# The second attention of a four-stage kernel: projections in halves between the heads, scores two heads at a time, loops written out

## The chip, the cores and the metric
The kernel runs on one core of one Trainium2 chip. The metric is device time in microseconds (us) of one execution. Engines: TensorE (PE), VectorE (DVE), ScalarE (ACT), GpSimd (POOL) and SyncE (SP), each with its own instruction stream; they order each other by semaphores.

## The reference
Two layers on x of 8 x 256 x 256 (batch, token, feature): recurrent scans, attentions and expert networks. The part that the change touches is the attention of the second layer, on the output of an LSTM scan, with 8 heads of 32 query and key features:

```python
xn = (x - mu) * jax.lax.rsqrt(var + LN_EPS) * gamma + beta
q = (xn @ Wq + bq).reshape(B, S, H, dk).transpose(0, 2, 1, 3)
k = (xn @ Wk + bk).reshape(B, S, H, dk).transpose(0, 2, 1, 3)
v = (xn @ Wv + bv).reshape(B, S, H, D).transpose(0, 2, 1, 3)
scores = jnp.einsum('bhsd,bhtd->bhst', q, k) / jnp.sqrt(jnp.asarray(dk, x.dtype))
p = jax.nn.softmax(scores, axis=-1)
att = jnp.einsum('bhst,bhtd->bhsd', p, v)
out = att.reshape(S, B, D, H).sum(axis=-1).reshape(B, S, D)
```

The last line sums eight neighbouring columns of the value product, so the kernel sums eight columns of `Wv` beforehand and a head's values have 32 columns.

## The kernel before, in words
`build_kernel` (L2058) runs `pipeline_one` (a scan of the first layer, its attention and experts, and the LSTM of the second layer), `attention_two` (L988), and `pipeline_two` (a gated scan and its experts). Only `attention_two` is touched.

**Precision.** Every float32 operand of a large product is split in two float16 parts, high and low (`_h`, `_l`, `_hi`, `_lo`); a product is three matmuls (high by high, and the two mixed ones). `split_matmul` (L98) issues six for two blocks of 128 contracted features.

**LayerNorm block (L1060 to L1175).** Four pieces of 512 columns: PE forms means and variances with a constant matrix, ACT squares and takes roots, DVE does the rest, POOL adds beta into `hs1`. DVE and ACT also split the projection weights. DVE's memsets stand at its start.

**A block between (L1186).** SP sets the semaphores to a start value for one batch that does not exist; PE writes 12 small matmuls into `pt` and `po`. The loops below begin with heads of that missing batch, so waits need no special case.

**The attention block (L1204 on).** Each engine runs `Fori(0, B)` over 8 batches, with the heads written out inside; waits compare with `at(b, per, k)`, computed in registers.

- PE, per head h: `scores` (L1273), six matmuls of 32 rows and 256 columns into `sc[h % 2]`; `turn` (L1285) of head h-1, four float32 transposes of the probabilities into `pt`; `values` (L1297) of head h-3, twelve matmuls of 32 columns into `po`. At h = 0, scores stand last. At h = 4, `project` (L1249) forms q, k and v of the next batch: 42 matmuls, six of them a bias over 2 rows, in three banks `pq`, `pk`, `pv`.
- ACT: `exps` (L1332), two exponentials with row sums; `high` (L1341), the float16 copy of the turned probabilities, of head h-2; at h = 0 the high parts of q and k, at h = 2 of v.
- DVE: the row maximum (L1412), negated into `nmax`; `low` (L1375), the remainder after `high`, of head h-2; at h = 0 the low parts of q and k and the reciprocals of the sums; at h = 2 `finish` (L1385) of the batch before, the low part of v, and `split_x` (L1369), two instructions that split the next batch's columns of `hs1` into `xn_h`, `xn_l`.
- POOL, beside them: twelve pieces of the next stage's weights, each a DMA, a scaling, a cast and a subtraction (L1214 to L1228).
- SP sends a finished batch to memory (L1243).

q, k, v, their parts and `xn` exist once, so q and k of a batch are read out at its start, after the last scores of the batch before.

## Time and profile before

| | us |
|---|---|
| median of 3 runs | 2952.01 |
| lowest and highest | 2944.11 and 2957.39 |
| the profiled execution | 2941.34 |
| its span, first to last instruction | 2939.5 |
| in the span: `pipeline_one` | 0 to 1417 |
| LayerNorm block and block between | 1417 to 1471.4 |
| attention block | 1471.4 to 1757 |
| `pipeline_two` | from 1761 |

Over the span PE is busy 2524.8 us (86%), DVE 1973.6 (67%), ACT 1149.9 (39%), POOL 430.8 (15%). The page's row of PE's granted clock reads 9 (0.9 or more of full speed) for most slices and falls to 5 and 6 around the second attention. Full speed is 2.4 GHz and 0.50 is 1.2 GHz, the two levels that occur; a figure between is a mean over time. Durations of matmuls overlap: the distance of two starts tells what one costs in a row of them.

### The profile page before, as it was taken

The numbers are of one execution on the slowest core, as the hardware profiler recorded it, in microseconds if no ns is written. First come the engines' busy times: TensorE is split into PE (matmuls) and PEld (weight loads), VectorE is DVE, ScalarE is ACT, GpSimd is POOL, SyncE is SP. The second block draws the span as 40 slices with busy tenths as digits, with TensorE's granted clock in tenths as the row PEclk, the third lists the DMA queues.
The fourth block names the chain that finished last, engine by engine and source line by source line (L and its number), as shares of the span: only waits on it lengthen the run. The fifth ranks groups of instructions, "written<-read, shape, count | busy, mean of one in ns | idle before, by whom it ended". The sixth has DMA issues, their size and how long they took to land. (4 is left out here: it accounts for less than half of the span.)

```text
span 2939.5 us, 119767 instructions
## 1 busy us (share of the span) xinstructions
PE 2524.8 (86%) x50858; PEld 2074.4 (71%) x50858; DVE 1973.6 (67%) x7388; ACT 1149.9 (39%) x3661; POOL 430.8 (15%) x404
## 2 busy tenths in 40 slices
PE   1678999999999999885377874899999999999999
PEld 0455677777777777643144543899999999999998
DVE  4557777777777777875745443667677666776665
ACT  3125555555555555562233432233333333333333
POOL 0000000000000000000189100122222222222222
PEclk9678999999999999997656565899999999999999
DMA  5000000000000000000122003000000000000000
GB/s 159 1 2 2 5 5 5 5 5 5 5 5 5 5 5 5 6 4 3 37 97 86 7 16 112 20 8 8 8 9 8 8 10 8 9 11 8 5 5 6
DMA packets 52730, 53.55 MB, mean 18 GB/s; under 512 B 24679, under 2 KB 46840, under 8 KB 50042
## 3 DMA queue, kind: packets, MB, share of 16 engines
q1 hardware_dynamic: 47284, 27.79, 3.5%
q0 software_dynamic: 2000, 14.68, 1.4%
q8 instruction: 390, 6.39, 0.9%
q10 hardware_dynamic: 2934, 3.69, 0.4%
q14 instruction: 122, 0.99, 0.1%
HBM read 39.59 MB, written 6.55 MB: 16 GB/s over the span
## 5 line engine op out<-in xcount | busy, mean ns | idle before, releaser
L103 PE MATMUL p<-g_hl,m_h 128*128 128x128 f16 x3072 | 529.2, 219 | 0.0
L103 PE MATMUL p<-g_hh,m_l 128*128 128x128 f16 x3072 | 529.1, 219 | 0.0
L103 PE MATMUL p<-g_hh,m_h 128*128 128x128 f16 x3072 | 529.1, 219 | 0.0
L765 DVE STREAM_TRANSPOSE gt<-lg_b 128x512 f32<-128x512 f32 x324 | 230.4, 711 | 217.0 <-PE lg_b L448 203.7
L1910 POOL TENSOR_TENSOR a_l<-a,a_h 128x384 f16<-128x384 f32 x256 | 234.1, 914 | 918.2 <-ACT a_h L1868 918.2
L657 ACT ACTIVATE hm<-xy,b 128x512 f32<-128x512 f32 x512 | 348.0, 680 | 0.1
L642 ACT ACTIVATE gl<-gt 128x128 f32<-128x128 f32 x324 | 100.2, 309 | 629.0 <-DVE gt L765 628.9
L103 PEld LDWEIGHTS p<-g_hh,m_h 128*128 128x128 f16 x3072 | 300.5, 98 | 1.8
L103 PEld LDWEIGHTS p<-g_hh,m_l 128*128 128x128 f16 x3072 | 300.7, 98 | 0.7
L103 PEld LDWEIGHTS p<-g_hl,m_h 128*128 128x128 f16 x3072 | 300.9, 98 | 0.0
L448 PE MATMUL lg_b<-a_wh_hi,lh 128*32 128x256 f16 x4096 | 217.7, 291 | 78.8 <-DVE lh L789 76.7
L448 PE MATMUL lg_b<-e_wh_hi,lh 128*32 128x256 f16 x4096 | 210.5, 283 | 46.3 <-DVE lh L789 45.6
L448 PEld LDWEIGHTS lg_b<-a_wh_hi,lh 128*32 128x32 f16 x4096 | 101.2, 100 | 160.4 <-DVE lh L789 129.3
L1794 PE MATMUL po<-m_h,a_h 128*128 128x256 f16 x768 | 208.4, 271 | 1.9 <-DVE acc L1949 1.9
L1794 PE MATMUL po<-m_h,a_l 128*128 128x256 f16 x768 | 209.0, 272 | 0.0
L1794 PE MATMUL po<-m_l,a_h 128*128 128x256 f16 x768 | 208.8, 272 | 0.0
L1858 ACT ACTIVATE cand<-g_b 128x16 f32<-128x16 f32 x256 | 47.1, 184 | 384.6 <-PE g_b L1758 384.6
L614 PE MATMUL yo<-hm,w2f 128*32 128x256 f32 x2048 | 161.9, 389 | 35.2 <-DVE tmp L815 35.0
L2024 DVE SCALAR_TENSOR_TENSOR zm<-zr,cand 128x16 f32<-128x16 f32 x256 | 44.4, 173 | 206.1 <-ACT cand L1858 205.0
L1868 ACT ACTIVATE a_h<-a 128x384 f16<-128x384 f32 x256 | 133.9, 523 | 105.8 <-DVE a L1933 105.8
L1736 PEld LDWEIGHTS g_b<-g_hh,gu_w 128*128 128x128 f16 x4096 | 136.7, 96 | 51.7 <-DVE g_hh L2029 46.5
L1736 PE MATMUL g_b<-g_hh,gu_w 128*128 128x8 f16 x4096 | 140.5, 166 | 37.1 <-DVE g_hh L2029 35.9
(421 smaller groups left out, 7105.5 us busy)
## 6 DMA issues: line engine op xcount, KB each, us to landing
m_stage<-in_m_w POOLq DMA_DIRECT2D x12, 1024.0 KB, 5.3
hs<-in_m_w SPq DMA_DIRECT2D x16, 384.0 KB, 3.2
xs<-in_x POOLq DMA_DIRECT2D x1, 2048.0 KB, 8.5
x_dram<-x SPq DMA_DIRECT2D x16, 128.0 KB, 2.2
s_v<-in_l_wv SPq DMA_DIRECT2D x1, 2048.0 KB
attention_dram<-att SPq DMA_DIRECT2D x16, 128.0 KB, 2.8
attr<-attention_dram SPq DMA_DIRECT2D x128, 16.0 KB, 1.8
x2r<-x_dram SPq DMA_DIRECT2D x16, 128.0 KB, 2.5
```

The source lines that it names most:

```text
L103: ins = pe.matmul(out, w[wp](k), x[xp](k), start=start, stop=last and k == KT - 1 and xp == 1, skip_group_check=True)
L448: last = pe.matmul(gate_block(ae, j, par), lh[:, part, ae, k, u, :], columns(w[name], k, j), start=False, stop=(part == 1 and k == KT - 1) ...
L614: last = pe.matmul(yo[q * HD:(q + 1) * HD, :, :], w2f[:, n % E1, :], tok[:, :, q, :], start=True, stop=True, skip_group_check=True, tile_p ...
L642: act.activation(gl[:, :].rearrange("p (m b) -> p m b", b=B), gt[:, :].rearrange("p (m n) -> p m n", n=32)[:, :, slot % QS * B:(slot % QS ...
L657: act.activation(hm32[:, n % 2, h * 512:(h + 1) * 512], xy[h][:, :], ACT.Gelu, bias=b1[:, n % E1:n % E1 + 1], scale=1.0 / S).then_inc(g_32, 1)
L765: dve.transpose(gt[:, :], lg_b[slot // QS % 2][:, :, :, :].rearrange("p g a x -> p (g a x)"))\
L1736: pe.matmul(o[:, slot % 8, m, :], w[:, k, m * P:(m + 1) * P], h(g_hh, k), start=False, stop=False, skip_group_check=True)
L1794: last = pe.matmul(po[:, half, :], x[:, n % 2, r], w[:, tl, :], start=(first and x is a_h and w is m3_h), stop=(end and x is a_l), skip_gr ...
L1858: act.activation(cand[:, :], g_b[slot // 8][:, slot % 8, 4:6].rearrange("p m b -> p (m b)"), ACT.Tanh, scale=1.0 / S).then_inc(u_act, 1)
L1868: act.activation(a_h[:, n % 2, :], a32[:, n % 2, :], ACT.Copy).then_inc(a_hi, 1)
L1910: pool.tensor_tensor(a_l[:, n % 2, :], a32[:, n % 2, :], a_h[:, n % 2, :], ALU.subtract).then_inc(a_lo, 1)
L2024: dve.scalar_tensor_tensor(out=zm[:, :], in0=zr[:, 0:16], scalar=1.0, in1=cand[:, :], op0=ALU.add, op1=ALU.mult).then_inc(z_mix, 1)
```

## The change
Loops over batches are written out, and waits compare with constants; the block between, its seeds and its dummy matmuls are gone, as is the projection of a ninth batch. Heads are numbered through, g = 0 to 63, in 32 pairs.

- `scores(p)` treats heads 2p and 2p+1: twelve matmuls, alternating between two row groups (r0 and r0 + 32) and two of four banks `sc`. It is issued in even heads.
- `project(b, j, half)` forms half of q, k or v (7 matmuls). `PROJECT_AT` puts the halves behind heads 0, 1, 3 (two), 5 and 6. All but the first batch use one bank, `pj`; a projection's first half waits for the low part of the one before (`pj_lo`).
- The bias matmuls contract over 128 rows, all but two of them zero.
- `xn`, q, k, v and their parts, and `sums`, are doubled; `split_x` works two batches ahead, high part at h = 4, low part at h = 6.
- ACT puts `high(g-1)` behind `exps(g)`; DVE has `low(g-2)` and the maximum of head g+2, before other work in odd heads and after it in even ones.
- In the LayerNorm block squares go to `prob`, `yy` to `att`, y replaces the root in place, seven memsets go and one of `brow` comes.

```diff
+GH = B * NH
+
+PROJECT_AT = {0: ((0, 0),), 1: ((0, 1),), 3: ((1, 0), (1, 1)), 5: ((2, 0),), 6: ((2, 1),)}
+HIGH_AT = {2: 0, 4: 1, 7: 2}
+PJ_SCALE = (float(DK) ** -0.5 / S, 1.0 / S, 1.0 / S)
...
-        brow = sb("brow2", [2, 3 * D], F16)
-        ones2 = sb("ones2b", [2, BT], F16)
+        brow = sb("brow2", [P, 3 * D], F16)
+        ones2 = sb("ones2b", [P, BT], F16)
...
-        nmax = sb("nmax", [P, 2, TT])
+        nmax = sb("nmax", [P, 4, TT])
         prob = sb("prob", [P, 2, TT, BT])
-        sums, rinv = sb("sums", [P, NH, TT]), sb("rinv", [P, NH, TT])
+        sums, rinv = sb("sums", [P, 2, NH, TT]), sb("rinv", [P, NH, TT])
         pt_h, pt_l = sb("pt_h", [P, 2, TT, BT], F16), sb("pt_l", [P, 2, TT, BT], F16)
...
-        sc = [ctx.enter_context(nc.psum_tensor(f"sc{j}", [P, TT, BT], F32)) for j in range(2)]
+        sc = [ctx.enter_context(nc.psum_tensor(f"sc{j}", [P, TT, BT], F32)) for j in range(4)]
         pt = [ctx.enter_context(nc.psum_tensor(f"pt{j}", [P, TT, BT], F32)) for j in range(2)]
         po = ctx.enter_context(nc.psum_tensor("po", [P, NH, TT, HV], F32))
-        pq, pk, pv = (ctx.enter_context(nc.psum_tensor(n, [P, TT, BT], F32)) for n in ("pq", "pk", "pv"))
+        pj = ctx.enter_context(nc.psum_tensor("pj", [P, TT, BT], F32))
+
+        def pj_bank(b, j):
+
+            return (sc[2], sc[3], pj)[j] if b == 0 else pj
...
+                dve.memset(brow[:, :], 0.0).then_inc(ready, 1)
                 dve.memset(ones2[:, :], 1.0)
-                dve.memset(hs1[:, :, (NI + 1) * CW:(NI + 1) * CW + B], 0.0)
-                dve.memset(sums[:, :, :], 1.0)
-                for tl in (prob, pt_h, pt_l):
-                    dve.memset(tl[:, :, :, :], 0.0)
-                for tl in (v_h, v_l):
-                    dve.memset(tl[:, :, :], 0.0)
...
+                    v, y = va[:, j % 2, :], root[:, j % 2, :]
...
-                        o = bank[:, m, :]
-                        pe.matmul(o, brow[0:2, j * D + m * P:j * D + (m + 1) * P], ones2[0:2, :], start=(m == 0),
-                                  stop=False, skip_group_check=True)
...
+            def project(b, j, half):
+
+                bank = pj_bank(b, j)
+                if half == 0:
+                    pe.wait_ge(xn_split, 2 * (b + 1))
+                    if b > 0:
+                        pe.wait_ge(pj_lo, 3 * b + j)
+                o, xh, xl = bank[:, half, :], xn_h[b % 2], xn_l[b % 2]
+                r = slice(half * P, (half + 1) * P)
+                if j < 2:
+                    n = "qk"[j]
+                    pe.matmul(o, brow[:, j * D + half * P:j * D + (half + 1) * P], ones2[:, :], start=(half == 0),
+                              stop=False, skip_group_check=True)
+                    last = split_matmul(pe, o, (lambda k: w_hi[n][:, k, r], lambda k: w_lo[n][:, k, r]),
+                                        (lambda k: xh[:, k, :], lambda k: xl[:, k, :]), False, last=True)
+                else:
+                    pe.matmul(o, ones2[:, 0:P], brow[:, 2 * D:3 * D], start=(half == 0), stop=False,
                               skip_group_check=True)
-                    w = (lambda k, u=u: xn_h[:, k, u * P:(u + 1) * P], lambda k, u=u: xn_l[:, k, u * P:(u + 1) * P])
-                    last = split_matmul(pe, o, w, (lambda k: w_hi["v"][:, k, :], lambda k: w_lo["v"][:, k, :]), False,
+                    last = split_matmul(pe, o, (lambda k: xh[:, k, r], lambda k: xl[:, k, r]),
+                                        (lambda k: w_hi["v"][:, k, :], lambda k: w_lo["v"][:, k, :]), False,
                                         last=True)
-                last.then_inc(proj_pe, 1)
...
+            def scores(p):
+
+                b, m, r = p // 4, p % 4 // 2, 2 * DK * (p % 2)
+                if p % 4 == 0:
+                    pe.wait_ge(pj_lo, 3 * b + 2)
+                if p >= 2:
+                    pe.wait_ge(exp_done, 2 * (2 * p - 2))
+                elif p == 1:
+                    pe.wait_ge(pj_lo, 3)
+                qh, ql, kh, kl = (v[b % 2] for v in (q_h, q_l, k_h, k_l))
...
+                    for q, k in ((qh, kh), (ql, kh), (qh, kl)):
+                        for e in range(2):
+                            r0 = r + e * DK
+                            last = pe.matmul(sc[2 * (p % 2) + e][:, s_, :], q[r0:r0 + DK, m, s_ * P:(s_ + 1) * P],
+                                             k[r0:r0 + DK, m, :], start=(s_ == 0 and k is kh and q is qh),
+                                             stop=(k is kl), skip_group_check=True, tile_position=(r0, 0))
                 last.then_inc(sc_pe, 1)
 
-            def turn(b, h):
-                pe.wait_ge(exp_done, at(b, 2 * NH, 2 * (h + 1)))
-                pe.wait_ge(pt_lo, at(b, NH, h + 1))
+            def turn(g):
+                pe.wait_ge(exp_done, 2 * (g + 1))
+                if g >= 2:
+                    pe.wait_ge(pt_lo, g - 1)
...
+                pe.wait_ge(pt_lo, g + 1)
                 if h == 0:
-                    pe.wait_ge(v_split, at(b, 1, 1))
-                    pe.wait_ge(att_done, at(b, 1, 1))
-                hd = h % NH
+                    pe.wait_ge(pj_lo, 3 * b + 3)
+                    if b > 0:
+                        pe.wait_ge(att_done, b)
+                vh, vl = v_h[b % 2], v_l[b % 2]
...
-            project(0)
-            with pe.Fori(0, B) as b:
-                for h in range(NH):
-                    if h > 0:
-                        scores(b, h)
-                    turn(b, h - 1)
-                    values(b, h - 3)
-                    if h == 0:
-                        scores(b, h)
-                    if h == 4:
-                        project(b + 1)
-            turn(B, -1)
-            for h in (-3, -2, -1):
-                values(B, h)
+            for j in range(3):
+                for half in range(2):
+                    project(0, j, half)
+            scores(0)
+            for g in range(GH + 2):
+                b, h = g // NH, g % NH
+                if 1 <= g <= GH:
+                    turn(g - 1)
+                if g % 2 == 0 and g // 2 + 1 < GH // 2:
+                    scores(g // 2 + 1)
+                if g >= 2:
+                    values(g - 2)
+                for j, half in PROJECT_AT.get(h, ()):
+                    if b + 1 < B:
+                        project(b + 1, j, half)
...
+            def exps(g):
+                b, h = g // NH, g % NH
+                act.wait_ge(neg_max, g + 1)
+                if g >= 2:
+                    act.wait_ge(t_pe, g - 1)
+                if h == 0 and b >= 2:
+                    act.wait_ge(r_done, b - 1)
...
+            def high(g):
+                act.wait_ge(t_pe, g + 1)
+                if g >= 2:
+                    act.wait_ge(pv_pe, g - 1)
+                act.activation(flat(pt_h[:, g % 2]), flat(pt[g % 2][:, :, :]), ACT.Copy).then_inc(pt_hi, 1)
+
+            def projected(b, j):
+                act.wait_ge(pj_full, 3 * b + j + 1)
+                if b >= 2 and j < 2:
+                    act.wait_ge(sc_pe, 4 * (b - 1))
+                elif b >= 2:
+                    act.wait_ge(pv_pe, NH * (b - 1))
+                act.activation(flat((q_h, k_h, v_h)[j][b % 2][:, :, :]), flat(pj_bank(b, j)[:, :, :]), ACT.Copy,
+                               scale=PJ_SCALE[j]).then_inc(pj_hi, 1)
...
+            for j in range(3):
+                projected(0, j)
+            for g in range(GH + 1):
+                b, h = g // NH, g % NH
+                if g < GH:
+                    exps(g)
+                if g >= 1:
+                    high(g - 1)
+                if h in HIGH_AT and b + 1 < B:
+                    projected(b + 1, HIGH_AT[h])
...
+            def split_x(b, part):
+
+                o = (LAG + 1) * CW
+                row = hs1[:, :, o:o + NCH * CW].rearrange("p k (t b) -> p k t b", b=B)[:, :, :, b]
+                if part == 0:
+                    if b >= 2:
+                        dve.wait_ge(pj_full, 3 * (b - 1))
+                    dve.tensor_scalar(xn_h[b % 2][:, :, :], row, 1.0, None, ALU.mult).then_inc(xn_split, 1)
+                else:
+                    dve.wait_ge(xn_split, 2 * b + 1)
+                    dve.tensor_tensor(xn_l[b % 2][:, :, :], row, xn_h[b % 2][:, :, :],
+                                      ALU.subtract).then_inc(xn_split, 1)
...
+            def projected(b, j):
+                dve.wait_ge(pj_hi, 3 * b + j + 1)
+                hi, lo = ((q_h, q_l), (k_h, k_l), (v_h, v_l))[j]
+                dve.scalar_tensor_tensor(out=lo[b % 2][:, :, :], in0=pj_bank(b, j)[:, :, :], scalar=PJ_SCALE[j],
+                                         in1=hi[b % 2][:, :, :], op0=ALU.mult, op1=ALU.subtract).then_inc(pj_lo, 1)
+
+            def row_max(g):
+                dve.wait_ge(sc_pe, g // 2 + 1)
+                if g >= 4:
+                    dve.wait_ge(exp_done, 2 * (g - 3))
+                dve.tensor_reduce(nmax[:, g % 4, :], sc[g % 4][:, :, :], AX_X, ALU.max,
+                                  negate=True).then_inc(neg_max, 1)
+
+            def low(g):
+                dve.wait_ge(pt_hi, g + 1)
+                dve.tensor_tensor(pt_l[:, g % 2], pt[g % 2][:, :, :], pt_h[:, g % 2], ALU.subtract).then_inc(pt_lo, 1)
...
+            split_x(0, 0)
+            split_x(0, 1)
+            for j in range(2):
+                projected(0, j)
+            row_max(0)
+            row_max(1)
+            projected(0, 2)
+            split_x(1, 0)
+            split_x(1, 1)
+            for g in range(GH + 2):
+                b, h = g // NH, g % NH
+                if 2 <= g:
+                    low(g - 2)
+                if g % 2 == 1 and g + 2 < GH:
+                    row_max(g + 2)
+                if h == 0 and b > 0:
+                    inverse(b - 1)
+                    if b < B:
+                        projected(b, 2)
+                elif h == 1 and b > 0:
+                    finish(b - 1)
+                elif h in (3, 5) and b + 1 < B:
+                    projected(b + 1, h // 2 - 1)
+                elif h in (4, 6) and b + 2 < B:
+                    split_x(b + 2, h // 2 - 2)
+                if g % 2 == 0 and g + 2 < GH:
+                    row_max(g + 2)
```

On PE, before, behind head 4 of a batch (`sc` scores, `pt` the turn, `po` values, `pq` the projection of q):

```order
L1280 MATMUL sc0<-k_h,q_h 128x256
L1280 MATMUL sc0<-k_h,q_l 128x256
L1280 MATMUL sc0<-k_l,q_h 128x256
...
L1291 MATMUL pt1<-ident2,prob 128x128 x4
L1307 MATMUL po<-v_h,pt_h 128x32
L1307 MATMUL po<-v_l,pt_h 128x32
...
L1251 ISA
L1257 MATMUL pq<-ones2b,brow2 128x256
L103 MATMUL pq<-xn_h,q2_hi 128x256
L103 MATMUL pq<-xn_h,q2_lo 128x256
```

and in the changed kernel, heads 4 and 5 of the first batch (`pj` here the first half of v of the second):

```order
L1285 MATMUL pt1<-ident2,prob 128x128 x4
L1273 MATMUL sc2<-k_h0,q_h0 128x256
L1273 MATMUL sc3<-k_h0,q_h0 128x256
L1273 MATMUL sc2<-k_h0,q_l0 128x256
L1273 MATMUL sc3<-k_h0,q_l0 128x256
...
L1303 MATMUL po<-v_h0,pt_h 128x32
...
L1285 MATMUL pt0<-ident2,prob 128x128 x4
...
L1251 MATMUL pj<-brow2,ones2b 128x256
L103 MATMUL pj<-v2_hi,xn_h1 128x256
```

The scores of two heads stand matmul by matmul beside each other and come once in two heads, and the projection is cut in pieces between heads.

On DVE, before, from head 2 to head 3 of a batch (`pt_l` the low part, `nmax` the row maximum):

```order
L1412 TENSOR_REDUCE nmax<-sc0 128x2
L1377 TENSOR_TENSOR pt_l<-pt0,pt_h 128x512
...
L1390 TENSOR_TENSOR att2<-po,rinv 128x512
...
L1418 SCALAR_TENSOR_TENSOR v_l<-pv,v_h 128x512
...
L1371 TENSOR_SCALAR xn_h<-hs1 128x512
L1372 ISA
L1373 TENSOR_TENSOR xn_l<-hs1,xn_h 128x512
...
L1412 TENSOR_REDUCE nmax<-sc1 128x2
```

and in the changed kernel, heads 3 to 6 of the first batch:

```order
L1392 TENSOR_REDUCE nmax<-sc1 128x2
L1385 SCALAR_TENSOR_TENSOR q_l0<-pj,q_h0 128x512
L1397 TENSOR_TENSOR pt_l<-pt0,pt_h 128x512
L1376 TENSOR_SCALAR xn_h1<-hs1 128x512
L1392 TENSOR_REDUCE nmax<-sc2 128x2
L1397 TENSOR_TENSOR pt_l<-pt1,pt_h 128x512
L1392 TENSOR_REDUCE nmax<-sc3 128x2
L1385 SCALAR_TENSOR_TENSOR k_l0<-pj,k_h0 128x512
L1397 TENSOR_TENSOR pt_l<-pt0,pt_h 128x512
L1379 TENSOR_TENSOR xn_l1<-hs1,xn_h1 128x512
```

The two x-split instructions no longer follow each other, and the low parts of q and k stand behind a row maximum.

## Rows read from the trace of the kernel before

**Rows 1.** Stretches, core 0: us, then busy us and instructions by engine, PEclk, DMA

```profile
core 0: us, PE busy (x) PEld busy (x) DVE busy (x) ACT busy (x) POOL busy (x), PEclk, DMA share, GB/s
...
1626.00:1660.00 34.00, 30.79 (x215) 19.80 (x214) 14.22 (x23) 12.11 (x39) 0.07 (x1) 0.50 0.05 8
...
1800.00:2939.50 1139.50, 1091.56 (x22474) 1044.27 (x22474) 774.64 (x3001) 352.79 (x1087) 234.10 (x256) 0.97 0.05 13
```

**Rows 2.** The same view, for projection, heads alone, heads afterwards, the whole stage

```profile
1643.00:1654.00 11.00, 11.00 (x47) 5.57 (x46) 0.52 (x1) 0.00 (x0) 0.00 (x0) 0.50 0.00 0
1699.00:1705.00 6.00, 6.00 (x48) 4.30 (x47) 4.58 (x7) 2.27 (x7) 0.00 (x0) 0.50 0.27 39
...
1746.70:1756.00 9.30, 6.88 (x108) 5.51 (x106) 5.53 (x9) 5.12 (x16) 0.00 (x0) 1.00 0.00 0
...
1471.40:1757.00 285.60, 227.50 (x1826) 151.02 (x1826) 138.15 (x190) 110.99 (x348) 144.97 (x48) 0.62 0.17 51
```

**Rows 3.** Waits from 1493 to 1748: us in total, times, longest

```profile
DVE nmax L1412 <- PE sc L1280: 115.7, 36, 12.1
```

**Rows 4.** Timeline of PE at 1.2 GHz: start, duration, line, out<-in, shapes

```profile
1667.71 0.39 PE L1280 MATMUL sc<-k_h,q_h 32*128 32x256 f16 x1
...
1668.76 0.42 PE L1280 MATMUL sc<-k_l,q_h 32*128 32x256 f16 x1
1669.10 1.11 PE L1291 MATMUL pt<-ident,prob 128*128 128x128 f32 x4
1670.01 0.23 PE L1307 MATMUL po<-v_h,pt_h 128*128 128x32 f16 x1
...
1670.47 0.39 PE L1280 MATMUL sc<-k_h,q_h 32*128 32x256 f16 x1
```

**Rows 5.** The same at 2.4 GHz, with DVE's row maximum

```profile
1746.75 0.28 PE L1280 MATMUL sc<-k_h,q_h 32*128 32x256 f16 x1
...
1747.50 0.66 PE L1291 MATMUL pt<-ident,prob 128*128 128x128 f32 x4
1747.70 0.69 DVE L1412 TENSOR_REDUCE nmax<-sc 128x2 f32<-128x512 f32 x1 [9.31 <-PE sc L1280]
...
1748.00 0.18 PE L1307 MATMUL po<-v_h,pt_h 128*128 128x32 f16 x1
...
1748.39 0.28 PE L1280 MATMUL sc<-k_h,q_h 32*128 32x256 f16 x1
```

**Rows 6.** Timeline of PE: the bias matmuls that begin a half of a projection

```profile
1738.67 0.39 PE L1257 MATMUL pq<-ones2b,brow 2*128 2x256 f16 x1
1740.38 0.39 PE L1257 MATMUL pq<-ones2b,brow 2*128 2x256 f16 x1
...
1744.80 0.28 PE L1266 MATMUL pv<-brow,ones2b 2*128 2x256 f16 x1
```

**Rows 7.** Timeline of PE in stage one, 2.4 GHz: blocks in four column groups

```profile
302.22 0.39 PE L448 MATMUL lg_b<-a_wh_lo,lh 128*32 128x256 f16 x8
302.44 0.39 PE L448 MATMUL lg_b<-a_wh_hi,lh 128*32 128x256 f16 x8
```

**Rows 8.** DVE's groups from 1471 to 1626: count, busy us, mean ns, idle before

```profile
L1373 DVE TENSOR_TENSOR xn_l<-hs,xn_h 128x512 f16<-128x512 f16 x4 | 14.8, 3709 | 0.1
L1371 DVE TENSOR_SCALAR xn_h<-hs 128x512 f16 x4 | 8.5, 2130 | 0.0
...
L1373 DVE TENSOR_TENSOR xn_l<-hs,xn_h 128x512 f16<-128x512 f32 x1 | 1.1, 1072 | 0.0
```

**Rows 9.** The same view from 1471 to 1757: the low part

```profile
L1377 DVE TENSOR_TENSOR pt_l<-pt,pt_h 128x512 f16<-128x512 f32 x66 | 45.1, 684 | 7.5 <-ACT pt_h L1344 7.5
```

**Rows 10.** Timelines: block between, attention's first and last on DVE, POOL's last

```profile
1469.67 1.01 PE L1198 MATMUL pt<-v_h,pt_h 128*128 128x128 f16 x8 [21.30 <-PEq L1020]
...
1471.41 0.62 DVE L1371 TENSOR_SCALAR xn_h<-hs 128x512 f16<-128x512 f32 x1 [3.91 <-PEq L1186]
...
1756.18 0.69 DVE L1390 TENSOR_TENSOR att<-po,rinv 128x512 f32<-128x512 f32 x1 [0.62 <-PE po L1307]
...
1622.00 4.07 POOL L1228 TENSOR_TENSOR m_l<-m_stage,m_h 128x2048 f16<-128x2048 f32 x1
```

More of the change, by code:

```diff
@@ L1239, in _ @@
             rows = attd[0:B * T * D].rearrange("(b h s p j) -> b p h s j", h=NH, s=TT, p=P, j=HV)
-            with sp.Fori(0, B) as b:
-                sp.wait_ge(att_done, at(b, 1, 2))
+            for b in range(B):
+                sp.wait_ge(att_done, b + 1)
                 for s_ in range(TT):
-                    sp.dma_start(rows[bass.ds(b, 1), :, :, s_, :].rearrange("o p h j -> (o p) h j"),
-                                 att[:, :, s_, :]).then_inc(att_sent, 16)
-            sp.wait_ge(att_sent, 16 * TT * (B + 2))
+                    sp.dma_start(rows[b, :, :, s_, :], att[:, :, s_, :]).then_inc(att_sent, 16)
@@ L1273, in scores @@
-            def scores(b, h):
-                r0, m = DK * (h % 4), h // 4
-                if h == 0:
-                    pe.wait_ge(qk_split, at(b, 2, 2))
-                pe.wait_ge(exp_done, at(b, 2 * NH, 2 * (h - 1)))
-                for s_ in range(TT):
-                    for q, k in ((q_h, k_h), (q_l, k_h), (q_h, k_l)):
-                        last = pe.matmul(sc[h % 2][:, s_, :], q[r0:r0 + DK, m, s_ * P:(s_ + 1) * P],
-                                         k[r0:r0 + DK, m, :], start=(s_ == 0 and k is k_h and q is q_h),
-                                         stop=(k is k_l), skip_group_check=True, tile_position=(r0, 0))
+                if half == 1:
+                    last.then_inc(pj_full, 1)
@@ L1303, in values @@
                 for s_ in range(TT):
-                    o = po[:, hd, s_, :]
+                    o = po[:, h, s_, :]
                     for u in range(TT):
-                        for pp, vp in ((pt_h, v_h), (pt_h, v_l), (pt_l, v_h)):
-                            last = pe.matmul(o, pp[:, h % 2, u, s_ * P:(s_ + 1) * P], vp[:, u, hd * HV:(hd + 1) * HV],
-                                             start=(h == 0 and s_ == 0 and u == 0 and pp is pt_h and vp is v_h),
+                        for pp, vp in ((pt_h, vh), (pt_h, vl), (pt_l, vh)):
+                            last = pe.matmul(o, pp[:, g % 2, u, s_ * P:(s_ + 1) * P], vp[:, u, h * HV:(h + 1) * HV],
+                                             start=(h == 0 and s_ == 0 and u == 0 and pp is pt_h and vp is vh),
@@ L1422, in _ @@
-            inverse(B)
-            low(B, -2)
-            low(B, -1)
-            finish(B)
+            split_x(0, 0)
[8 more added lines that the diff above has]
+            for g in range(GH + 2):
+                b, h = g // NH, g % NH
+                if 2 <= g:
[14 more added lines that the diff above has]
+                    row_max(g + 2)
```

146 lines of the change are left out of this document (28 added, 118 removed).

## The prediction
> **What bounds the kernel now.** I first read the table of stages, to see which part of the span the change touches. The second attention runs from 1471.4 to 1756.9 us [rows 10], 285.5 us of 2939.5; everything else keeps its instructions. In a stretch as long as a batch, 1626 to 1660, TensorE (PE) is busy 30.8 us of 34, VectorE (DVE) 14.2, ScalarE 12.1 [rows 1]. The granted clock there is 0.50 of full speed, and 0.62 over the stage [rows 2]: 1.2 GHz for three quarters of the time and 2.4 GHz for one quarter. Second, the waits: from 1493 to 1748 DVE stood 115.7 us before its row maximum, for PE's scores [rows 3]. That puts PE's own order in front: each score block is followed by a turn, the values of an older head, and once a batch by a projection in one piece, with nobody having work for the maximum meanwhile.
>
> Third, the timeline, for the price of a head on PE. At 1.2 GHz: scores start at 1667.71, the turn at 1669.10, values at 1670.01, the next scores at 1670.47, so 1.39 + 0.91 + 0.46 = 2.76 us [rows 4]. At 2.4 GHz: 0.75 + 0.50 + 0.39 = 1.64 us [rows 5]. Half a q, k or v projection (7 matmuls) takes 1.71 us at 1.2 GHz (1738.67 to 1740.38) and 0.98 at 2.4 (two from 1744.80 to 1746.75) [rows 5, 6]; six make 10.3 and 5.9 us. So a batch is 8 x 2.76 + 10.3 = 32.4 us at the low clock, 19.0 at the high one, against about 34 observed: PE is the limit for most of it, and waits in the rest.
>
> **What the change does to PE's work.** (a) Scores of two heads alternate between two 32-row groups and two banks. The trace of before has no two row groups in flight. Its nearest rows are column groups: eight 256-column matmuls in four column groups start and are over in 0.22 us at 2.4 GHz (302.22 to 302.44) [rows 7]. Serial ones start 0.21 apart at 1.2 GHz (five steps from 1667.71 to 1668.76 [rows 4]), so 0.107 at 2.4, and eight would take 0.86. Four groups thus ran fully at once. Ends for the row groups: side by side, a pair costs what one head costs now (1.39 / 0.75 us); one after the other, twice that. I take side by side, the column groups being the nearest thing; the other end is a rival.
>
> The Trainium skill (TensorE: Matmul & The Clock Gate, Part 3: Packing small matmuls) gives four row groups a measured gain of 3.07, not 4, and says the groups run at once only if their row groups differ. No run shows it yet; an estimate by that page would leave a pair 0.65 of the serial time, 0.38 us more than I take, about 12 us over the stage, still inside my forecast's spread.
>
> (b) The bias matmuls contract over 128 rows in place of 2, so the array keeps one layout. Seven matmuls at 0.213 are 1.49 us where 1.71 stood; at 2.4 GHz 0.77 for 0.98. (c) Before projects nine times, the ninth for nothing; now eight.
>
> Sum for a batch at 1.2 GHz: 4 x 1.39 + 8 x 0.91 + 8 x 0.46 + 6 x 1.49 = 25.5 us. At 2.4 GHz: 3.0 + 4.0 + 3.1 + 4.6 = 14.7 us.
>
> **What waits remain.** Two kinds. In an even head PE runs turn, scores, values; DVE's queue has the next row maximum before that turn's low part, so the low part comes after scores (0.95 us from their first matmul to the maximum at 2.4 GHz, 1746.75 to 1747.70, which is the block's 0.75 and 0.2; so 1.59 at 1.2 GHz), maximum (about 0.60) and low part (0.69): 2.9 us at the low clock, against 2.76 of PE work, a loss near 0.1 for each of two pairs without projection. At the high clock the chain binds: 0.95 + 0.60 + 0.69 + 0.39 + 0.50 = 3.13 us a pair [rows 5]. Then one bank (`pj`) serves all three projections: at heads 3 and 5 PE may start k, or v, only when DVE has finished the low part of the one before, behind a row maximum: 0.60 + 0.61 + about 0.1 after the low part that values wait for, less 0.46 of values, 0.85 us, twice a batch. So 25.5 + 1.7 + 0.1 = 27.3 us at the low clock. High: four pairs 12.5, the four halves in odd heads 3.1 (the halves at heads 0 and 6 lie in the wait), the bank 1.6: 17.2 us. DVE and ScalarE keep their work a batch, some 14 and 12 us [rows 1] in operations such as the low part's 0.684 [rows 9]: under 17.2, so neither leads by its load.
>
> **GpSimd holds DVE.** While GpSimd splits the weights of the next stage (until 1626), the mean x split is 2.13 + 3.71 us, where 0.62 + 1.07 is its length alone [rows 8, 10]: 4.1 us more. Before pays this in four batches, as one block, with PE idle behind it. Now the halves stand at heads 4 and 6, but fall on six batches and one at the start. The slack of DVE against PE (3.4 a head against 2) covers the first half and some 1.5 us of the second; I put 15 us for all, ends 0 (all covered) and 29 (7 x 4.1).
>
> **The clock.** What the rows show: with one projection after another PE was at 1.2 GHz for all of 1643 to 1654; heads without projection filled it 6.0 of 6.0 us at 1.2 GHz too (1699 to 1705); after the last projection had brought 2.4 GHz, heads kept it, at 6.9 of 9.3 us busy, to the end [rows 2]. The clock fell in before where q and k were split at a batch's start and PE stood. The change takes out the long stream that raised it, and also the gap that ended it. I take the share of before, 0.62, so 24% of the time at 2.4 GHz; both ends, all low and all high, are rivals. Rate: 0.76 / 27.3 + 0.24 / 17.2 batches a us, 23.9 us a batch.
>
> **The rest.** The LayerNorm block loses seven memsets and gains one of 128 rows; they lie in DVE's wait for the first mean. Its chain keeps order and lengths: y is now computed in place. The block between, with 12 matmuls and semaphore seeds, goes with one barrier: from 1469.67 to 1471.41 [rows 10], 1.7 us. Loops written out: no address arithmetic; the code is fetched at some 9 matmuls a us, and stage three, also written out, gets 22474 in 1139.5 us, 20 a us [rows 1], so I cost the code at nothing; were it late, PE would show it as idle time for issue. The twelve GpSimd passes stay, and end at 1626 (1622.00 + 4.07) [rows 10], a floor.
>
> Sum: first split 1.8, 8 x 23.9 = 191.2, GpSimd's hold 15, last high, low, values and finish 3 more than PE's own: 211. Against 285.5 and with 1.7 at the start: 76 us less. The profiled execution took 2941.3 us (span 2939.5 and 1.8 around it), so 2865 for it; the median of the three runs is 2952.0, 10.7 above. I predict the median: **2876 us**.
>
> **Rivals.**
> *Clock high.* The batches follow without a gap, so once PE reaches 2.4 GHz it stays. 1.8 + 8 x 17.2 + 5 for a low first projection + 15 + 3 = 162, ending at 1632, just over GpSimd's floor: 125 less, 2827 us. For it: the last 9.3 us of rows 2. Against it: DVE's holds of 5 us.
> *Clock low throughout.* 1.8 + 8 x 27.3 + 15 + 3 = 238: 49 less, 2903 us. For it: no stream over 3 us is left, and heads filled PE at 1.2 GHz with no rise.
> *Row groups one after another* (the change does not do what it says): 5.6 us a batch more at the low clock, 3 at the high one: 32.9 and 20.2, 28.6 mixed, 37 us more than forecast, 2913 us.
> *Slower: every change of row group drains the array*, as the change from 32 to 128 rows does now: last scores matmul to turn is 0.34 (1668.76 to 1669.10 [rows 4]) where 0.21 is a matmul, so 0.13 lost. Twelve changes a pair, 48 a batch: 32.9 + 6.2 = 39.1 us. Such gaps go with the low clock: 1.8 + 8 x 39.1 + 18 = 333, 45 more, 2997 us. It decides from 0.05 us a change on (8 x 48 x 0.05 = 19, on top of 283, is 285.5 + 1.7 + 0.5% of the time). Against it: column groups show no such gap.
>
> **How the numbers follow.** Forecast 0.40, clock high 0.25, clock low 0.20, row groups serial 0.08, drains at the low clock 0.04, gains eaten by holds and waits I have not seen 0.03 (no change). The range 2822 to 2918 holds the first four but for their edges, the ends 0 and 29 of the hold, and the run-to-run spread of 7 us. Half a percent, 15 us, is about what a measurement tells from no change. Faster 0.93, within it 0.03, slower 0.04.
>
> **What would show it.** Pairs of scores matmuls starting together and a block of twelve taking 1.4 us (0.75) confirm (a). Seven projection matmuls in 1.5 us confirm (b). PE idle before a k or v projection near 0.85 us confirms the bank; x splits of 4 to 5 us with PE idle behind the second, the hold. The stage's mean clock decides among the first three. I am wrong if the stage ends after 1730, or if a wait for ScalarE leads.

## The result and the profile after

The changed kernel takes **2811.3 us** (median of 4 runs, 2809.5 to 2814.6) beside 2952.9 of the kernel before: a ratio of **0.9525**, 95% interval 0.9501 to 0.9549. The forecast was 2876, range 2822 to 2918: the sign is right, but the gain is 142 us where 76 were forecast, and the time lies outside the range.

The stretch view first (us, busy us and instructions of PE, its weight load, DVE, ScalarE, GpSimd, then PEclk, DMA): the attention, and three batches of it.

```profile
1468.70:1633.00 164.30, 132.86 (x1744) 102.92 (x1744) 127.39 (x184) 107.17 (x346) 145.67 (x48) 0.90 0.31 90
1505.10:1522.90 17.80, 14.87 (x221) 11.97 (x219) 16.07 (x24) 13.19 (x44) 17.17 (x7) 1.00 0.28 76
1522.90:1543.90 21.00, 18.07 (x221) 13.75 (x219) 17.91 (x23) 13.15 (x44) 20.12 (x8) 0.84 0.39 114
1543.90:1563.30 19.40, 16.58 (x221) 12.85 (x219) 15.28 (x23) 13.19 (x44) 18.50 (x8) 0.91 0.26 70
```

The stage takes 164.3 us at a mean clock of 0.90; before it was 285.5 at 0.62 [rows 2, 10]. Of the 121 us, 95 are busy time of PE (132.9 us, not 227.5) and 27 its idle time. From `finish` to `finish`, the batches take 17.8, 21.0, 19.4, 17.8, 21.0, 19.2 us. The same 221 matmuls take 17.8 us where the clock stays at 2.4 GHz, and 1.6 us more for each of its falls to 1.2 GHz, which last 3 to 4 us (six in these six batches).

Waits from 1490 to 1620 (us in total, times, longest), to be read against [rows 3]:

```profile
ACT pt_h L1344 <- PE pt L1285: 42.6, 28, 3.8
DVE nmax L1392 <- PE sc L1273: 22.7, 17, 4.0
...
PE po L1303 <- DVE pt_l L1397: 8.0, 15, 1.3
...
PE pj L1246 <- DVE q_l L1385: 5.7, 7, 0.8
PE pj L1251 <- DVE k_l L1385: 5.7, 7, 0.8
```

The maximum's wait for scores is 22.7 us in these 130, where it was 115.7 in 255. PE's own waits are for DVE: the low part before values, and the one bank's read-out, 0.82 us twice a batch.

How the two profiled executions differ: the stage begins 2.8 us earlier, is 121.2 us shorter, and what follows takes 1179.6 us, not 1182.7: 126.9 us in all, from 2939.5 to 2812.6. The profiled run of before lay 11.6 us under its median, that of after 3.3 above; that is the other 15 us of the 142.

### The profile page after: what moved, and what is told of

It reads as the page before. It is cut to its first block and busy times, and to the rows that moved or that the text cites. A ratio compares the mean times of both kernels' runs of the same rounds, so it can differ in the third digit from the quotient of the medians.

```text
span 2812.6 us, 119114 instructions
## 1 busy us (share of the span) xinstructions
PE 2424.7 (86%) x50764; PEld 2022.1 (72%) x50764; DVE 1965.6 (70%) x7376; ACT 1144.6 (41%) x3659; POOL 431.1 (15%) x404
```

## Experiments

Times are medians, ratios stand against the kernel before on the same chip. Stage: from the first x split to the last `finish` of the profiled run. e5_pool_late and e12_low_late had one run each, and are read for their stage alone.

| run | time | ratio, 95% interval | stage, clock |
|---|---|---|---|
| changed kernel | 2811.3 | 0.9525 (0.9501, 0.9549) | 164.3, 0.90 |
| e1_bias2 | 2845.2 | 0.9656 (0.9620, 0.9693) | 191.8, 0.82 |
| e2_serial | 2841.8 | 0.9640 (0.9605, 0.9675) | 184.8, 0.84 |
| e3_gap | 2840.9 | 0.9640 (0.9603, 0.9676) | 185.7, 0.83 |
| e6_all3 (e1, e2, e3 together) | 2866.2 | 0.9724 (0.9693, 0.9754) | 214.1, 0.73 |
| e9_block | 2887.0 | 0.9802 (0.9773, 0.9830) | 234.0, 0.71 |
| e13_block_all | 2935.0 | 0.9921 (0.9897, 0.9944) | 287.4, 0.52 |
| e4_before_bias128 | 2918.5 | 0.9896 (0.9861, 0.9931) | 262.2, 0.66 |
| e5_pool_late | 2963.7 | | 165.5, 0.88 |
| e7_pool_quarters | 2823.6 | 0.9574 (0.9541, 0.9607) | 165.6, 0.88 |
| e8_low_first | 2807.7 | 0.9531 (0.9496, 0.9566) | 156.5, 0.93 |
| e12_low_late | 2940.9 | | 144.4, 0.96 |
| e10_low_xact | 2807.1 | 0.9533 (0.9502, 0.9564) | 148.4, 0.96 |
| e15_act_scale | 2799.9 | 0.9479 (0.9467, 0.9492) | 150.9, 0.94 |
| c_after_again | 2819.6 | 0.9580 (0.9546, 0.9614) | 164.3, 0.90 |
| c_after_five | 2814.4 | 0.9544 (0.9520, 0.9569) | 164.2, 0.90 |

The last two are the changed kernel again, the first beside e9, e10 and e12, the second beside e13 and e15. Its stage came out at 164.2 to 164.3 us each time. Its whole time moves by 8 us from chip to chip, and its ratio from 0.9525 to 0.9580, further than the 0.4% that was expected of the first repeat. So differences under 0.6% between runs on different chips say nothing.

> The changed kernel itself, to have it on the same chip and beside the same runs as the next ones; the ratio to the kernel before should be within 0.4% of the 0.9525 measured first. If the x splits meet GpSimd's operations at other points, the stage may be a few us off 164.3.

> The changed kernel itself beside e15_act_scale, for a difference of a few us on the same chip: 0.9525 to 0.958 of the kernel before, as measured so far, with the stage at 164.3 us and clock 0.90.

### What holds the clock: one property undone at a time

**Bias over 2 rows again.**

```diff
-                    pe.matmul(o, brow[:, j * D + half * P:j * D + (half + 1) * P], ones2[:, :], start=(half == 0),
+                    pe.matmul(o, brow[0:2, j * D + half * P:j * D + (half + 1) * P], ones2[0:2, :], start=(half == 0),
```

> The changed kernel with its bias matmuls over 2 rows again. Theory A (a projection whose matmuls all use 128 rows is what brings TensorE to 2.4 GHz within 3 us, as at 1470.43 to 1473.2 of the changed kernel; the projections of the kernel before, broken by a matmul over 2 rows in every seven, ran 10 us and more at 1.2 GHz): the clock of the stage falls from 0.90 to under 0.80 and the time grows by 20 us or more over 2811. Theory B (the 128 rows save only their 0.21 us a half projection): clock 0.88 to 0.92, 48 halves x 0.21 = 10 us at most, more likely 3 to 6, since part of it lies in waits: 2814 to 2817.

Measured 34 us more and a clock of 0.82, near theory A (which wanted under 0.80). Where a fall of the clock lasted 3 to 4 us, three now last 10 (from 1568.1, 1592.0 and 1615.9). The plainest sign is the first projection: it began at 1469.7 us, and the clock rose only at 1496.4, where in the changed kernel it rose 2.9 us after the projection's start. The first batch alone is 12 of the 27.5 us that the stage lost. Part of the loss is not the clock: the x splits met GpSimd longer, 51.0 us in all against 28.2. In the kernel before, the same edit alone (brow cleared to 128 rows, both matmuls over them) tells the sign:

> The kernel before with one edit, bias matmuls over 128 rows. Theory A (2-row matmuls within the stream keep the clock low): its projections reach 2.4 GHz within some 3 us of their start, the clock of the stage rises from 0.62 to 0.75 or more, and the time falls by 30 us or more under 2953. Theory B (only 0.21 us a half): 54 halves x 0.21 = 11 us at 1.2 GHz, clock 0.60 to 0.65: 2941 to 2945.

It won 1.0% (interval 0.7 to 1.4): 32 us beside the kernel before on the same chip, which is theory A's size and far over the 11 us of 54 halves; 23 us of it show in the profiled stages, with the x splits 5 us longer. The mean clock only went to 0.66, near theory B's range. But theory A's mechanism is there: in each of the nine projections the clock rose, 2.0 to 4.8 us after the start. In the kernel before it rose in or just behind seven of nine, 3.3 to 11.3 us after the start, and through the other two it stayed at 1.2 GHz, from 1590.3 to 1682.5 [rows 1, 2]. One projection of e4_before_bias128, which starts at 1629.7, up to the rise and behind it (columns as above):

```profile
1629.70:1634.40 4.70, 4.70 (x29) 3.33 (x26) 0.00 (x0) 0.60 (x1) 0.00 (x0) 0.50 0.00 0
1634.40:1641.20 6.80, 6.44 (x72) 5.04 (x71) 2.61 (x4) 2.76 (x10) 0.00 (x0) 1.00 0.00 0
```

The clock fell again in every batch, 7 to 10 us later, and stayed down for 17 to 24 us until the next projection. By itself the bias is not what brought 0.90.

**Scores head after head.**

```diff
-                for s_ in range(TT):
-                    for q, k in ((qh, kh), (ql, kh), (qh, kl)):
-                        for e in range(2):
+                for e in range(2):
+                    for s_ in range(TT):
+                        for q, k in ((qh, kh), (ql, kh), (qh, kl)):
```

> The changed kernel with the twelve scores matmuls of a pair in the order of the heads, six of one, then six of the other, so that no two neighbours use different row groups (but for the one place where the heads change). Theory A (side by side is worth its full half): each pair takes 0.6 us more at 2.4 GHz, 32 pairs 19 us, and as VectorE waits for the scores, 12 to 19 us reach the end: 2823 to 2830. Theory B (the time is set by VectorE and its chain, the scores lie in slack): under 5 us. A second question: if more matmuls one after another keep PE at the high clock, the loss could be smaller; the clock of the stage says so (0.90 now).

30 us more, past the 12 to 19 of theory A, yet the block of twelve took only 1.80 us at 1.2 GHz (1567.21 to 1569.01), not the 2.7 that twelve in a row would (11 steps of 0.21 and 0.34 to the next work). The timeline of PE in this run (start, duration, line, names, shape):

```profile
1567.21 0.39 PE L1273 MATMUL sc<-k_h,q_h 32*128 32x256 f16 x1
1567.40 0.42 PE L1273 MATMUL sc<-k_h,q_l 32*128 32x256 f16 x1
1567.62 0.42 PE L1273 MATMUL sc<-k_l,q_h 32*128 32x256 f16 x1
1567.62 0.39 PE L1273 MATMUL sc<-k_h,q_h 32*128 32x256 f16 x1
1567.81 0.42 PE L1273 MATMUL sc<-k_h,q_l 32*128 32x256 f16 x1
1567.83 0.42 PE L1273 MATMUL sc<-k_h,q_h 32*128 32x256 f16 x1
```

Two series, 0.21 us apart within each, and the second begins with the third matmul of the first: PE starts the other head's matmuls, on other rows, before those ahead of them in the program. So at 1.2 GHz a pair takes only 0.41 us more than the 1.39 of alternating heads (at 2.4 GHz 0.24), 8 to 13 us over 32 pairs; the rest of the run's 30 us is clock (0.84) and x splits (9.3 us longer).

**The gap at a batch's start.**

```diff
-                    pe.wait_ge(exp_done, 2 * (2 * p - 2))
+                    pe.wait_ge(exp_done, 2 * (2 * p - (0 if p % 4 == 0 else 2)))
```

> The changed kernel, where the first pair of scores of a batch waits until the last exponentials of the batch before, so that a gap of PE comes back at the batch's start, some 2 to 3 us long. Theory A (it was the gap at the start of a batch that ended the high clock in the kernel before, and without it the high clock stays): the clock of the stage falls towards 0.65, each of 7 batches loses the gap and 5 us or more of low clock: 50 us or more, 2860 and up. Theory B (a gap costs itself and the clock comes back within 3 to 4 us, as it does behind the x splits of the changed kernel at 1482.8): 7 x 3 = 20 us or less and clock over 0.80.

The gap came back as 1.69 us of idle PE:

```profile
1520.44 0.28 PE L1273 MATMUL sc<-k_h,q_h 32*128 32x256 f16 x2 [1.69 <-ACT prob L1337]
```

30 us more, clock 0.83, between the theories, nearer B: 7 x 1.7 is 12, the x splits took 12 more, and the falls of the clock lasted 3 to 10 us. The gap alone does not throw a whole batch to 1.2 GHz.

**All three, and the projection in one place.**

> The changed kernel with three of its properties undone at once: bias over 2 rows, scores head after head, and the gap at a batch's start. Each alone took the clock of the stage from 0.90 to 0.82 to 0.84 and cost 34, 30 and 30 us. Theory A (the clock has a point of decision, and what is undone together pushes it over: the mean clock goes to the 0.62 of the kernel before): clock under 0.72 and a loss of 94 us or more over 2811: 2905 or more. Theory B (the three share one loss, an occasional drop of the clock that any of them brings): clock about 0.80, 2850 to 2870.

The clock went to 0.73 and the time to 2866: less than the sum of the three. Theory B's range, though its clock (0.80) was too high; theory A fell. Something else kept the clock over the 0.62 of before. The next run moves the projection:

```diff
-PROJECT_AT = {0: ((0, 0),), 1: ((0, 1),), 3: ((1, 0), (1, 1)), 5: ((2, 0),), 6: ((2, 1),)}
+PROJECT_AT = {4: ((0, 0), (0, 1), (1, 0), (1, 1), (2, 0), (2, 1))}
```

(ScalarE and DVE read all three out at head 4, too.)

> The changed kernel with the projection of a batch in one place again, all six halves at head 4 through the one bank. PE has to wait twice in it for the read-out (about 0.8 to 1.6 us each: high part 0.6, low part 0.6 and the way between). Theory A (spread halves keep PE dense between the heads, and without them the six heads that have none lose the clock): the clock falls under 0.75, the stage grows by 45 us or more, of them some 7 x 3 for the waits. Theory B (where the projections stand does not matter for the clock): clock 0.85 to 0.92, only the waits are paid: 15 to 25 us more.

Theory A: clock 0.71, stage 69.7 us longer. 32 us of it are idle time of PE (63.5 us, not 31.4): two waits of 1.50 us a batch inside the block, and longer ones behind it for the low part before values (3.13 us at 1539.24). The other 38 are PE's busy time, 170.6 us for the same 1744 matmuls and not 132.9; that is the clock. It is the largest effect of one property. The stage, and the stretch of a batch behind its block, heads alone:

```profile
1470.00:1704.10 234.10, 170.56 (x1744) 119.02 (x1744) 133.63 (x184) 111.60 (x346) 143.89 (x48) 0.71 0.21 63
...
1540.60:1555.70 15.10, 14.26 (x155) 9.45 (x155) 10.69 (x15) 9.54 (x31) 14.62 (x5) 0.50 0.46 137
```

PE is busy 14.3 of 15.1 us, on scores side by side, turns and values, and stays at 1.2 GHz. In the trace's record of the clock, six of the nine rises lie within a block (1529.0 for one). The other three, at 1587.0, 1645.1 and 1692.9, lie in heads alone, 12 to 21 us after the last matmul of a projection. One of them:

```profile
1635.00:1645.10 10.10, 10.06 (x106) 6.78 (x104) 6.79 (x12) 7.60 (x26) 0.00 (x0) 0.50 0.17 28
1645.10:1658.70 13.60, 7.89 (x96) 6.06 (x92) 5.54 (x9) 4.94 (x15) 0.00 (x0) 1.00 0.00 1
```

So heads alone can raise the clock, but late and not each time, where the projections raised it within a few us. A last run takes block, 2-row bias and head order together:

> The changed kernel with the projection in one place (head 4), the bias over 2 rows, and the scores head after head: the three that made PE's stream between projections what it was before. What is left of the change: no gap at a batch's start, double buffers, loops written out, eight projections. Theory A (these three carry the whole difference of the clock): clock 0.55 to 0.64, as 0.62 before, and with its waits in the block a time of 2930 or more, near the kernel before. Theory B (a fourth thing, such as the double buffers, also keeps the clock): clock 0.70 or more as with the block alone (0.71), and under 2905.

```profile
1468.10:1755.50 287.40, 226.76 (x1744) 139.89 (x1744) 138.87 (x184) 111.45 (x346) 143.70 (x48) 0.52 0.17 51
1600.00:1612.40 12.40, 12.37 (x122) 8.31 (x118) 6.69 (x12) 6.56 (x22) 12.25 (x4) 0.50 0.31 94
```

The clock is 0.52, lower than in either theory and than before: it rose in the block at 1546.3, for 7 us, and once more in heads at 1751.1, for 3. The time, 2935.0, is theory A's. With these three undone the stage is as long as before, 287.4 us, though with waits for the one bank (21 us) that the kernel before did not have. So the three are enough to account for the clock: projection spread, 0.90 to 0.71, bias and row groups on top of it, 0.71 to 0.52. Their effects are not independent: e1, e2 and e3, each taken from the full change, cost 21 to 28 us of stage, together 50, and the block 70.

### What the x splits and the one bank cost

```diff
+                pool.wait_ge(att_done, B)
```

> The changed kernel, but GpSimd's twelve passes over the next stage's weights begin only when the attention is over, so that no x split meets them. The end of the kernel comes later for that (the next stage waits for these weights) and is not the question; the stage alone is read. Theory A (a hold costs its own time in DVE's queue and the low clock after the stall of PE): every x split takes 0.62 and 1.07 us (1.5 and 2.0 on average now), the clock of the stage rises from 0.90 to 0.97 or more, and the stage falls from 164.3 to about 140 us, 8 batches of 17.2 and 3. Theory B (the holds lie in VectorE's slack): the stage keeps within 5 us of 164.

Theory B: with x splits of 0.62 and 1.07 us (13.5 us in all, not 28.2) the stage is not shorter, 165.5 us. The six full batches take 116.2 us, as in the changed kernel, and 17.8 each where the clock does not fall: there the holds lay in DVE's slack. In the first batch PE idles less by nearly 3 us, but the clock falls twice more (1492.5 and 1499.4).

And with GpSimd's operations in quarters, each of the three like this one:

```diff
-                pool.tensor_scalar(w, w, S / 2, None, ALU.mult).then_inc(m_split, 1)
+                for a, z in cuts:
+                    pool.tensor_scalar(w[:, a:z, :], w[:, a:z, :], S / 2, None, ALU.mult).then_inc(m_split, 1)
```

> The changed kernel with each of GpSimd's 36 operations cut in four (1.35, 0.5 and 1.0 us each in place of 5.4, 1.9 and 4.1). In the trace of the changed kernel an x split that meets a GpSimd operation ends 0.35 to 0.86 us after that operation's end. Theory A (the hold lasts until the running GpSimd instruction ends, then VectorE gets in): the mean of the two x splits falls from 1.5 and 2.0 to under 1.2 and 1.7, fewer stalls of PE, the clock rises above 0.92, and the time falls by 5 to 15 us. Theory B (GpSimd keeps the access from one instruction to the next): the splits are no shorter, and GpSimd's own end comes later by its overhead a piece; 2811 or a few us more.

The splits fell to 0.79 and 1.26 us, as theory A has it, but its clock over 0.92 and its gain did not come: clock 0.88, stage 165.6, and GpSimd ended at 1641.7, 17.6 us later than in the changed kernel, so that the next stage waited (1187.7 us behind the stage, not 1179.6). What bound the stage instead shows in the changed kernel's timeline of PE, heads 3 to 5 of a batch:

```profile
1547.17 0.19 PE L1303 MATMUL po<-v_h,pt_h 128*128 128x32 f16 x1 [0.51 <-DVE pt_l L1397]
1548.46 0.37 PE L1246 MATMUL pj<-ones2b,brow 128*128 128x256 f16 x1 [0.82 <-DVE q_l L1385]
...
1554.34 0.19 PE L1303 MATMUL po<-v_h,pt_h 128*128 128x32 f16 x1 [0.51 <-DVE pt_l L1397]
...
1555.63 0.27 PE L1251 MATMUL pj<-brow,ones2b 128*128 128x256 f16 x1 [0.82 <-DVE k_l L1385]
```

Two idle times close together, and the clock falls at the end of the second (1548.4). The pair stands 14 times in the stage, with the same two lengths, and the clock fell behind six of them; what decides between them is open. An order takes the second away, the low part of q or k before the row maximum in heads 3 and 5:

```diff
-                if g % 2 == 1 and g + 2 < GH:
+                if g % 2 == 1 and g + 2 < GH and not (h in (3, 5) and b + 1 < B):
                     row_max(g + 2)
...
                     projected(b + 1, h // 2 - 1)
+                    row_max(g + 2)
```

> The changed kernel, where in heads 3 and 5 VectorE makes the low part of q, or k, before the row maximum and not behind it, so that PE may start the next projection earlier (it waits 0.82 us at 1490.0 for that low part). Theory A (the one bank costs what it shows as waits, 5.7 us in 7 times each for the k and v projections): 14 x 0.6 = 8 us less at most, as the row maximum and what follows comes 0.6 later: 2803 to 2808. Theory B (the row maximum is the tighter path and the bank's wait is only moved): no change or up to 8 us more.

The wait per projection fell from 0.82 to 0.2 us and the stage to 156.5, 7.8 less: theory A inside the stage. Only one fall is left behind the first batch, 10 us from 1532.6. In the whole kernel the ratio (0.9531) can't be told from the changed kernel's. Both causes out together:

> The changed kernel with the low parts of q and k first and GpSimd's passes after the attention, so that neither the wait for the one bank nor a hold is left; only the stage is read (the kernel's end comes later, since the next stage waits for the weights). Theory A (it was these two that brought the low clock in the changed kernel; each alone left the other): clock 0.97 or more behind the first batch, stage 140 to 146 us. Theory B (the clock falls at other short waits, such as the 0.5 us for the low part before values): clock under 0.94, stage over 152.

```profile
1469.30:1613.70 144.40, 124.12 (x1744) 98.31 (x1744) 113.03 (x184) 107.23 (x346) 1.17 (x2) 0.96 0.13 29
1502.60:1519.20 16.60, 14.87 (x221) 11.98 (x219) 14.05 (x24) 13.21 (x44) 0.00 (x0) 1.00 0.12 19
```

Stage 144.4 us, each full batch 16.6 us, the clock never down after 1487. Theory A. Now the holds do count: with the bank's wait gone, they are 156.5 less 144.4, 12.1 us; with it they were nothing. Some 9 of the 12 are idle time of PE (29.4 us in the stage, not 20.3), so here the holds cost mainly their own waits. The bank's wait is worth 7.8 us with holds and 21.0 without, and of these 21, 8 are idle time (28.7 us, not 20.3) and the rest the clock.

### A version faster than both

Beside the order of e8, ScalarE takes the high part of the x split:

```diff
+                if h == 5 and b + 2 < B:
+                    act.wait_ge(pj_full, 3 * (b + 1))
+                    act.activation(xn_h[b % 2][:, :, :], hs1[:, :, o:o + NCH * CW].rearrange(
+                        "p k (t b) -> p k t b", b=B)[:, :, :, b + 2], ACT.Copy).then_inc(xn_split, 1)
```

> The changed kernel with the low parts of q and k made before the row maximum (as in the run before, whose stage took 156.5 us at clock 0.93), and the high part of the x split made by ScalarE, so that VectorE meets GpSimd once a batch and not twice. Theory A (each stall of PE that goes takes a stretch of low clock with it): the clock rises over 0.95 and the stage ends near GpSimd's own end, 1626, not before: 5 to 8 us under the control run. Theory B (ScalarE's 0.6 us a batch comes into the chain of the probabilities and takes back what VectorE gains): no change against the control.

Stage 148.4, clock 0.96. The whole is 12.5 us under the control's median beside it, but the intervals of the ratios overlap. The attention ended at 1620.5; GpSimd at 1627.2, and the next stage began behind GpSimd:

```profile
1623.11 4.06 POOL L1215 TENSOR_TENSOR m_l<-m_stage,m_h 128x2048 f16<-128x2048 f32 x1
1628.48 0.10 POOL L1542 MEMSET s_one<- 1x8 f32 x1 [1.31 <-POOLq L996]
```

So ScalarE scales the last weight piece in quarters:

```diff
+                if b == B - 1 and 2 <= h <= 5:
+                    act.wait_ge(m_staged[1], 16 * 6)
+                    w = m_stage[1][:, 4 * (h - 2):4 * (h - 1), :]
+                    act.activation(w, w, ACT.Copy, scale=S / 2).then_inc(m_scaled, 1)
```

> The run e10_low_xact (stage 148.4 us, ended 1620.6, while GpSimd's last pass ended 1627.2 and the next stage began behind it) with one more edit: ScalarE scales the last of the twelve weight pieces, in four quarters behind heads 2 to 5 of the last batch, so that GpSimd ends 5.4 us sooner. Theory A (GpSimd's end is now what the next stage waits for): GpSimd and attention end together near 1621, 5 us less than e10_low_xact, and some 12 to 17 us less than the changed kernel beside it. Theory B (the next stage is not held by GpSimd's end but by something fixed behind it): no change against e10_low_xact.

```profile
1612.31 1.89 POOL L1216 CAST m_h<-m_stage 128x2048 f16<-128x2048 f32 x1 [1.04 <-ACT m_stage L1370]
1614.28 4.07 POOL L1218 TENSOR_TENSOR m_l<-m_stage,m_h 128x2048 f16<-128x2048 f32 x1
1621.82 0.09 POOL L1549 MEMSET s_one<- 1x8 f32 x1 [3.47 <-POOLq L996]
```

GpSimd ended at 1618.3, the attention at 1618.5, and the floor was real: what follows takes 1180.1 us again, not 1186.0. The stage grew by 2.5 us for it, nearly all in the last batch. 2799.9 us, 14.5 under the changed kernel beside it (2814.4), and the two intervals don't meet. This is the fastest version.

## Why the forecast was wrong

By the prediction's steps:

- **Row groups side by side: right.** Twelve scores matmuls start in six pairs 0.11 us apart at 2.4 GHz (first pair 1476.49), a block takes 0.76 us there (1552.12 to 1552.88), and 1.39 at 1.2 GHz (from e9_block, 1540.61 for one), as forecast. The four-group loss of the Trainium skill (TensorE: Matmul & The Clock Gate, Part 3: Packing small matmuls), from which the prediction estimated 0.38 us a pair more, does not show with two groups.

```profile
1476.49 0.28 PE L1273 MATMUL sc<-k_h,q_h 32*128 32x256 f16 x2
1476.61 0.27 PE L1273 MATMUL sc<-k_h,q_l 32*128 32x256 f16 x2
1476.72 0.27 PE L1273 MATMUL sc<-k_l,q_h 32*128 32x256 f16 x2
```

- **Bias over 128 rows: size right, effect missed.** A half projection takes 1.47 us (1470.43 to 1471.90) and 0.77 (1473.34 to 1474.11), forecast 1.49 and 0.77. That it also lets the clock rise sooner (e4_before_bias128: nine of nine projections) stood nowhere.
- **The bank's wait: right, 0.82 for 0.85.** That the clock falls with it was missed.
- **A batch at 2.4 GHz: nearly right.** 17.8 us against 17.2.
- **GpSimd's hold: 15 us put in, 0 found.** Its lower end was right for this kernel. The splits were indeed 14.7 us longer in all than alone, but PE's wait for the one bank, and DVE's own slack, covered it.
- **The clock: the step that failed.** "I take the share of before, 0.62" gave 23.9 us a batch; the stage ran at 0.90, and six full batches average 19.4. Over eight batches that is 36 us, with the hold's 15 more than the whole 47 that the stage was over-estimated (211 against 164.3; the rest of the sum, a first projection in part at 1.2 GHz among it, was a few us short). The prediction read its rows rightly, heads did not raise the clock in them and a gap ended it, but it took a share that belonged to the old order for a constant. What the runs show in its place is how soon after a fall the clock comes back. With a projection once a batch and a bias over 2 rows it stayed down for 20 us and more at a time (from 1488 to 1512 for one, and once for 92 us, through two projections). With projections in pieces every few heads and a bias over 128 rows it came back in 3 to 4 us, but for one fall of 7 in the first batch. The change made both of these. A reason for the rival "clock high" stood there, it gave 162 us for the stage, 2 short; it got 0.25.
- **Start and end.** Start 2.8 us earlier for 1.7; other runs of the changed kernel begin at 1464.9 to 1468.7, so this is within their spread. GpSimd's end (1624.05) lay below the stage's, as forecast.
- **The median.** 10.7 us were added because before's profiled run lay that much under its median. That was a property of one run and not of the kernels: after's profiled run lay 3.3 us above its median. It is 14 us of the error of 65.
- **Rivals.** Row groups serial: not so; its price can't be had by an order alone, since PE overlaps them anyway. Drains at a change of row group: none, pairs alternate at 0.11 us.

Left open: how much of e1 to e3 is clock and how much x splits that met GpSimd at other times, since each run shifts both; and why the order of the scores and a gap of 1.69 us lengthen the falls, which no run takes apart.

## What to carry to other kernels

Treat TensorE's clock as an outcome of the order. Ask, for each fall, which work raises it again and how far away that work stands. Here it was the projections, dense matmuls over all 128 rows, and dealt out evenly they were worth more than their own time. That one decision, taken back alone, cost 70 us of the 121 that the stage had won, 38 by the clock and 32 by waits that the block brought with it.

When two kinds of wait overlap, take both out before judging either. Here the holds alone were worth nothing and the bank's wait alone 7.8 us, both together 19.9. And before shortening a stage, look at what runs beside it: here GpSimd's end lay 9 us ahead of the stage's, and became the end of it.

## What the chip showed that was not expected

- PE fully busy does not mean a high clock. Over heads alone it stayed at 0.50 with PE busy 12.37 of 12.4 us (e13_block_all), and three times it rose over heads alone (e9_block). It was 1.00 over batches with PE busy 14.87 of 16.6 us, where projections stood between the heads (e12_low_late). In the changed kernel the first projection raised it 2.9 us after its start (1470.43 to about 1473.3), from a PE idle for 23 us.
- Matmuls on other rows start before those ahead of them: the second head's first matmul at 1567.62, with the first head's third.
- VectorE's x split is held to the end of one instruction of GpSimd and hardly longer. In the changed kernel twelve splits were held; eleven end 0.35 to 0.87 us behind the end of a GpSimd instruction, and one, a low part against a scaling, 0.86 us before it (1517.12). In e1_bias2:

```profile
1586.11 5.85 DVE L1376 TENSOR_SCALAR xn_h<-hs 128x512 f16<-128x512 f32 x1
1586.23 5.38 POOL L1211 TENSOR_SCALAR m_stage<-m_stage 128x2048 f32<-128x2048 f32 x1
```

The one ends at 1591.96, the other at 1591.61; by the record VectorE's had begun first, by 0.12 us, and was held all the same. The Trainium skill (SBUF — State Buffer, section SBUF: two separate sides) has VectorE and GpSimd share a pair of ports that is locked for a whole instruction; by it, smaller instructions of GpSimd shorten the hold, and the quarters did so (means 0.79 and 1.26 us, from 1.49 and 2.04). They made GpSimd itself slower: four times 128x512 took 5.85 to 6.62 us where one of 128x2048 took 5.38.
